# A transformer block with soft experts: the second expert weight eight rows to a partition, the first layer's units in steps of eight columns

## What is computed

```python
xn = rmsnorm(x, norm_gamma)
sn = rmsnorm(slot_embeds, slot_norm_gamma)
logits = jnp.einsum('bnd,esd->bnes', xn, sn)
dispatch = jax.nn.softmax(logits, axis=1)
combine = jax.nn.softmax(logits.reshape(b, n, e * s), axis=-1)
slots = jnp.einsum('bnd,bnes->besd', xn, dispatch)
h = jnp.einsum('besd,edh->besh', slots, w1) + b1[None, :, None, :]
h = jax.nn.gelu(h, approximate=False)
eo = jnp.einsum('besh,ehd->besd', h, w2) + b2[None, :, None, :]
out = jnp.einsum('bmd,bnm->bnd', eo.reshape(b, e * s, DIM), combine)
```

## Time and profile before

| | us |
|---|---|
| median of 3 runs | 3712.88 |
| lowest and highest run | 3712.85, 3720.46 |
| the profiled execution | 3718.94 |
| its span, first to last instruction | 3717.1 |
| PE busy | 3225.0 (87%) |
| DVE busy | 2254.6 (61%) |
| ACT busy | 1844.5 (50%) |

### The profile page before, as it was taken

One profiled execution on the slowest core, in us unless ns is written; L12 is line 12 of the kernel. 1 busy time (PEld: TensorE's weight loads), 2 busy tenths in 40 slices (PEclk: granted clock), 3 DMA queues, 4 the chain that ended last, 5 costly groups with the idle time before them and its releaser, 6 DMA issues.

```text
span 3717.1 us, 45336 instructions
## 1 busy us (share of the span) xinstructions
PE 3225.0 (87%) x17663; PEld 1563.5 (42%) x17663; DVE 2254.6 (61%) x4305; ACT 1844.5 (50%) x3423; POOL 258.1 (7%) x143
## 2 busy tenths in 40 slices
PE   4679998899869999889887999988897799997999
PEld 2323333346643333244753333325475233333457
DVE  3668777364558877556265878637536587773632
ACT  1246665556215666546412666654641466664551
POOL 2200000110400000011030000001112000000100
PEclk9789998899989999899998999989999899998999
DMA  5312100105420220001532011000353110101042
GB/s 113 101 25 36 33 4 1 46 14 192 140 58 1 36 36 1 24 23 49 189 120 47 5 32 36 1 24 23 102 166 101 35 35 11 27 1 40 6 139 100
DMA packets 123190, 202.01 MB, mean 54 GB/s; under 512 B 9604, under 2 KB 106632, under 8 KB 119868
## 3 DMA queue, kind: packets, MB, share of 16 engines
q1 hardware_dynamic: 112016, 186.43, 18.2%
q10 hardware_dynamic: 10960, 12.68, 1.3%
HBM read 156.14 MB, written 42.16 MB: 53 GB/s over the span
## 4 chain that ended last, share of the span: by engine, by line
PE 68%; DVE 12%; DMA 8%; ACT 5%; issue 2%; SPq 2%; POOL 1%; DVEq 0%; ACTq 0%
PE ps L654 14%; PE ps L634 11%; PE ps L568 9%; PE ps L768 6%; DVE pm L1168 6%; PE ps L581 5%; DMA R<-nrow 5%; PE ps L742 4%; DMA R<-in_L_ffn_w_dram 2%; PE ps L784 2%; PE ps L528 2%; PE ps L794 2%; PE ps L619 2%; ACT R L909 1%; SPq L432 1%
## 5 line engine op out<-in xcount | busy, mean ns | idle before, releaser
L1168 DVE TENSOR_REDUCE pm<-ps 128x1 f32<-128x512 f32 (+4 forms) x2560 | 1400.9, 604 | 445.7 <-PE ps L568 305.9
L909 ACT ACTIVATE R<-ps 128x512 f32<-128x512 f32 (+1 forms) x2240 | 1185.5, 587 | 829.4 <-PE ps L634 675.0
L634 PE MATMUL ps<-R 99*128 99x512 bf16 (+3 forms) x2560 | 839.1, 363 | 159.1 <-DMA R<-nrow 146.9
L654 PE MATMUL ps<-R 128*17 128x512 f32 (+3 forms) x5120 | 616.1, 556 | 18.1 <-ACT R L903 16.6
L568 PE MATMUL ps<-R 96*128 96x512 bf16 x1536 | 590.5, 395 | 35.5 <-DVE pm L1168 32.7
L634 PEld LDWEIGHTS ps<-R 99*128 99x128 bf16 x2560 | 240.9, 99 | 402.3 <-DMA R<-nrow 158.0
L568 PEld LDWEIGHTS ps<-R 96*128 96x128 bf16 x1536 | 148.2, 98 | 486.6 <-DVE pm L1168 385.8
L768 PE MATMUL ps<-R 128*128 128x512 f32 x512 | 233.4, 614 | 13.0 <-ACT R L993 13.0
L581 PE MATMUL ps<-R 128*128 128x257 f32 x1024 | 237.1, 387 | 4.1 <-ACT R L858 3.6
L742 PE MATMUL ps<-snT,R 128*128 128x512 f32 x512 | 229.8, 594 | 6.3 <-ACT R L939 6.3
L581 PEld LDWEIGHTS ps<-R 128*128 128x128 f32 x1024 | 197.3, 194 | 42.2 <-issue 12.3
(11 more groups left out here) (153 smaller groups left out, 3383.9 us busy)
## 6 DMA issues: line engine op xcount, KB each, us to landing
R<-in_L_ffn_w_dram SPq DMA_DIRECT2D x64, 1024.0 KB, 7.0
R<-q_parts SPq DMA_DIRECT2D x12, 768.0 KB
R<-k_parts SPq DMA_DIRECT2D x12, 768.0 KB
R<-in_L_attn_x_dram SPq DMA_DIRECT2D x16, 512.0 KB, 8.1
q_parts<-R SPq DMA_DIRECT2D x16, 512.0 KB, 5.0
k_parts<-R SPq DMA_DIRECT2D x16, 512.0 KB, 4.6
R<-in_L_attn_x_dram SPq DMA_DIRECT2D x4, 2048.0 KB, 8.2
x_park<-R SPq DMA_DIRECT2D x16, 512.0 KB, 2.6
```

The lines of the kernel that those rows point to most:

```text
L634: last = mm(bank[:, i * w:(i + 1) * w], kst[g % 2][0:BROWS, h0 + i, j * P:(j + 1) * P], qst[g % 2][0:BROWS, h0 + i, (c + 1) * CH - w:(c + ...
L654: last = mm(ps[32 * h:32 * h + VC, 6, CH - w:CH], vall[:, j, HG * g + h, :], Eb[s % ESLOTS][:, h, 0:w], start=j == 0, stop=True, skip_grou ...
L909: A(Eb[s % ESLOTS][:, h0:h0 + n, 0:w], ps[:, u % NST, 0:n * w].rearrange("p (n w) -> p n w", n=n), ACT.Exp, scale=SCALE).then_inc(s_ex, 1)
L1168: mx = lambda o, i: V.tensor_reduce(o, i, AX.X, ALU.max)
```

## The change

`w2` is loaded so that partition p holds the eight successive rows 8p to 8p + 7, which makes one run of 8 KB per partition out of eight runs of 1 KB. Step j on partition p now stands for hidden unit 8p + j. So `hidden` takes for step j the columns j, j + 8, j + 16, ... of `w1s`: the same 128 columns' worth of weight per step, but neighbouring ones lie 8 elements (32 bytes) apart. `w1` is loaded as before. The bias table follows: `b1` is loaded as 8 rows of 1024 (4 KB each) into a part of R1, PE transposes it in 8 steps with every eighth column, and ACT's bias column is `j * E + e`.

```diff
-        pb1 = view(R2, 7424, 128)
+        pb1 = view(R1, 14336, HID).rearrange("e (p j) -> e p j", j=JH)
...
-                    sp.dma_start(w2s[e % NR], w2[e].rearrange("(j p) d -> p j d", p=P)).then_inc(s_ew[e % NR], 16)
+                    sp.dma_start(w2s[e % NR], w2[e].rearrange("(p j) d -> p j d", p=P)).then_inc(s_ew[e % NR], 16)
...
-            tr(ps[:, 7, 0:E * JH], pb1[0:E * JH, :], ident[0:E * JH, 0:E * JH]).then_inc(s_pt, 1)
+            for j in range(JH):
+                last = tr(ps[:, 7, j * E:(j + 1) * E], pb1[0:E, :, j], ident[0:E, 0:E])
+            last.then_inc(s_pt, 1)
...
-                                      w1s[e % NR][:, k, j * P:(j + 1) * P], slotsT[:, k, e * P:(e + 1) * P],
+                                      w1s[e % NR][:, k, :].rearrange("p (m j) -> p m j", j=JH)[:, :, j], slotsT[:, k, e * P:(e + 1) * P],
...
-            act.dma_start(pb1[0:E * JH, :], b1.rearrange("e (j p) -> (e j) p", p=P)).then_inc(s_w2, 16)
+            act.dma_start(pb1[0:E, :, :].rearrange("e p j -> e (p j)"), b1).then_inc(s_w2, 16)
...
-                                 bias=b1T[:, e * JH + j:e * JH + j + 1])
+                                 bias=b1T[:, j * E + e:j * E + e + 1])
```

## The result

The changed kernel's median is 3809.07 us (3802.80 to 3814.93, 4 runs) against 3716.67 for the kernel before in the same comparison. The ratio is 1.0247, with a 95% interval from 1.0221 to 1.0273. I had forecast 3708.3; the time came out within 6 us of the first rival, the loads that slow down in full (3803.7), and 3 us above the end of my range.

The account below looks back on a forecast made before the run. PE was taken as the bound, with 18.5 us of waits for a weight in reach; 3.0 us from the transfer plus 1.6 from the clock made 4.6 us off, 3708.3 against the median, range 3701 to 3806.

Parts of the forecast that it names:

- the first rival: First-layer weight loads slow down in full, +111 ns for each of 1024; net +90.8 us, 3803.7 us; chance 0.20.
- What bounds the stage: In the expert stage PE's first layer waits 12 times for a weight, 18.5 us in all, before experts 3, 5 and 7.
- The transfer: The second weight's load in 8 KB runs lands 0.3 us sooner each time, 3.0 us off the waits in all.
- The clock behind the waits: Two first layers ran slow behind long waits, 3.2 us; shorter waits remove half of it, 1.6 us.
- The weight loads: The first layer's 1024 loads with columns 32 bytes apart cost nothing more: taken as zero.
- The bf16 row: Prices a first-layer weight load with gaps from a bf16 operand's load: 136 ns instead of 111, +25 ns, an upper end.
- The transposes' row: Prices a first-layer weight load with gaps from the transposes' load: 235 ns instead of 111, +124 ns, an upper end.
- The little price: Rival: first-layer weight loads grow by 25 ns each, 25.6 us, net +9.8 and 3722.7 us; chance 0.13.
- No sooner: Rival: the second weight lands no sooner in 8 KB runs, all waits stay, 3712.9 us; chance 0.12.

Follow-up runs that it names:

- the split: The kernel before with a semaphore of its own for the second weight, so the first layer waits for the first weight alone; 3698.90 us, ratio 0.9952.
- The run with ACT's block cut in two: The split with ACT's four exponentials between Gelu 3 and Gelu 4 divided, two moved behind Gelu 5; 3689.77 us, ratio 0.9931 against the kernel before.

## Why the prediction was wrong

**What bounds the stage** held: PE with 18.5 us of waits for the second of two transfers. That they were just this was shown by the split, which removed them.

**The transfer** had the right sign and place, and half the size. 0.3 us per load was measured as 0.6; the term of 3.0 us was 7.5 us of waits less 1.7 for ACT, 5.8. I had taken the rate of the 4 KB runs, 414 GB/s, and given 8 KB nothing beyond it; real weights moved at 449, which is the upper end that I gave (0.5 us), and the landing came 0.1 sooner still.

**The clock behind the waits** I counted with 1.6 us. In the run with the transfer alone both slow stretches were gone from the profiled execution (3.2 us), but one more of its four stages than before began with a long one (below, 1.2). The run came out 7.5 us lower by the medians, 3.7 to 11.5 by its interval, which the 7.4 that 5.8 and 1.6 make fits; so would anything from 4 to 11.

**The weight loads** are the step that failed: "I take zero: the plain load runs at half the pace in columns of the transposes, so it has every second slot of the port free". The load grew from 192 to 335 ns, and a MATMUL from 112 to 235 ns from start to start, 1024 times: +126 us where the term said 0. The step took the transposes' pace in columns for a pace that 32-bit matmul weights could reach with a line per column. They can't: the table gives 1.81 to 1.84 ns per line for every distance from 2 to 4. The pace in columns says nothing of the pace in lines. A contiguous load has four columns per line and asks for a line every 3.5 ns; with a gap it asks every 0.865 and gets one every 1.83. The bf16 row, which I preferred as nearest, is of another kind of load, as the 62 ns of bf16 weights at distance 8 show. The transposes' row is of another kind as well, so it is luck that my upper end from it, 235 ns, is the measured 235: it took their 59 ns for 32 lines as 1.83 ns per line, but transposes at distance 8 get 128 lines in 112 ns. Whatever their 59 ns are spent on, it isn't that price, and I know of no reason why the two figures agree. The rule that I had cited against the change, from the Trainium skill's page "SBUF — State Buffer", section "Door 1: The DMA port swizzle (why `[64,N]` ≈ `[32,N]`)" (at least two accesses per line), had the right sign, and the two runs at distance 2 and 4 agree with it. The transposes don't: with two columns to a line their loads take 209 ns, no less than with one.

**The first rival** predicted +90.8 us; the expert stages grew by 91.5. The four stages last 65.25, 66.80, 67.07 and 65.01 us before, 89.12, 89.12, 89.12 and 88.25 after, by the starts of the first layer and the ends of the last second layer. But the agreement hides two errors. It took twice the load's time, +111 ns, where it was +123, which makes 126.1 us and not 113.4. And it missed two discounts. One is the clock at the start of each stage, which it counted nowhere. The first two first layers of batch 0, before and after, and PE's clock in them:

```profile
880.21 9.04 PE L784 MATMUL ps<-R 128*128 128x128 f32 x64 [3.20 <-DVE R L1347]
...
880.20:884.20 4.00, 3.99 (x21) 3.99 (x22) 3.45 (x17) 4.00 (x3) 0.00 (x0) 0.57 1.09 351
```

```profile
882.00 15.53 PE L786 MATMUL ps<-R 128*128 128x128 f32 x64 [3.19 <-DVE R L1349]
...
882.00:886.00 4.00, 4.00 (x17) 4.00 (x17) 3.36 (x16) 4.00 (x3) 0.00 (x0) 0.50 1.07 344
```

Behind DVE's 3.2 us the granted clock is at its lower level, 1.2 GHz, for 3 to 4 us in the first and for 6 us in the second. Before, that costs 9.1 - 7.1 = 2.0 us; after, 15.4 - 15.0 = 0.4, for the long load doesn't get slower with the clock: 17 MATMULs in 4 us are 235 ns each at 0.50 as at 1.00. Over the four batches the two first layers took 9.1, 10.3, 9.0 and 9.0 us before, and 15.4 each time after, which gives back 8.8 - 1.4 = 7.4 us. The other is that every stop of PE costs some 0.3 us beyond the wait itself: a first layer between two waits takes 3.84 us from its start to its end, against 3.57 where it runs on without either. The run with ACT's block cut in two, which has none of the 14 stops, bears that out. Its four stages last 59.31, 59.34, 59.26 and 58.40 us, 27.8 less than before; the waits are 19.4 of that, the slow stretches behind them 3.2, the starts of the stages 0.9, and 4.3 are left, 0.3 per stop. So 126.1 - 22.6 - 7.4 - 4.3 = 91.8, against 91.5 measured.

**The little price** would have needed +25 ns where 123 came; it was worked out from a bf16 load, which pays less still (6 ns). **No sooner** fell with the run of the transfer alone, with 369, 414 and 449 GB/s at 1, 4 and 8 KB. The Trainium skill's page "DMA: Bandwidth & Descriptors", section "Specifications", which puts the full rate at 512 bytes per run, doesn't hold for this kernel.

The span grew by 96.0 us, of which 91.5 are the expert stages; the other 4.5 lie in the stretches between them (880.21 to 882.00 us before the first, for one), and the bias path alone didn't show them. Two executions of one kernel differ by as much, and the start of the first stage lies anywhere from 875.7 to 883.1 us in the runs shown here, so I leave them unexplained.

## What to carry to other kernels

Count the 16-byte lines that an operand of PE touches, per partition: with 32-bit matmul weights or a moving operand each costs some 1.8 ns (measured with 128 weight columns), so two columns to a line are nearly free and one to a line takes a MATMUL from 112 to 235 ns, unless 512 moving columns stand beside the load. Don't take that price from another kind of load, nor to another: bf16 weights and transposes had prices of their own here. Before a layout is changed to make a transfer faster, look at which semaphore holds the consumer: here the wait was for a weight that the waiting step doesn't read, and a second semaphore gave 18 us without touching the layout. And when a wait is removed, look for what is late next; cutting ACT's block in two gave another 9 us.

## What the hardware showed that I had not expected

- With one weight column to a line, a MATMUL follows the other every 235 ns at a granted clock of 0.50 as at 1.00, so half the clock cost the changed kernel next to nothing there.
- The operand with gaps pays alike on either side (stationary 233 ns, moving 226 at 16 bytes), and both at once, at 32 bytes, cost 243, hardly more than the 238 of one.
- With bf16 weights a line per column costs 6 ns per matmul (56 to 62), with transposes 3 to 12 (109 to 112 at a distance of 32 bytes, 121 at 16). A transpose's load is no shorter with two columns to a line (209 ns) than with one (212 and 193).
- A stop of PE in the expert stage cost 0.3 us beyond the wait itself (4.3 us for 14 stops).
- Transfers moved 369 GB/s in runs of 1 KB, 414 in runs of 4 KB and 449 in runs of 8 KB, with all DMA engines busy in each.
- The price isn't quite flat: 267 ns at a distance of 48 bytes and 218 at 64, the same in two executions. The cause is open.
